# A weight load released by GpSimd, behind a drain, instead of by TensorE

## The chip, the cores and the metric

The kernel runs on one core of one Trainium2 chip. The metric is the device time of one execution in microseconds (us). Three runs of the kernel before took 1146.43, 1149.06 and 1155.12 us, so its time is the median, 1149.06 us.

## What is computed

One decoder layer on x of 8 x 256 tokens with 512 features, all in float32: attention with a window mask, a long convolution over a second input, and a mixture of experts. Only the last part matters here. In the reference, shortened:

```python
idx, wts = _router(x, gate_w, e_bias)            # 64 experts, 6 for each token
shared = _relu2(x @ shared_up_w.T) @ shared_down_w.T
# routed: each expert takes at most CAP = 128 tokens
h  = _relu2(einsum('ecd,eid->eci', xd, w1))      # 512 -> 256
yd = einsum('eci,edi->ecd', h, w2)               # 256 -> 512
out = x + shared + zeros((T, D)).at[tok].add(y_assign)
```

## The kernel before

The program is written engine by engine: each engine has its own list of instructions in the order in which it runs them, and semaphores tie the lists together. Nothing is planned at run time.

The expert stage is the last one. It handles 64 experts, one by one, in eight passes of a loop over UE = 8 experts (s is the place in the pass, i the pass). For each expert n = 8 i + s:

- SyncE (SP) issues one load of the expert's weights, 1 MB, into slot n mod 4 of the ring `wring` (NW = 4 slots). The line is 382.
- GpSimd (POOL) gathers the 128 token rows of the expert from `token_rows` into a ring of eight slots with an indirect DMA (line 515), eight experts ahead of their use.
- TensorE transposes the token rows (line 1466), multiplies them with the first weights (`hidden`), waits for ReLU and square, and multiplies with the second weights (`outputs`). Its order in a step is `tokens_T` of the expert after next, `hidden` of the next expert, `outputs` of this one, and in four of the eight steps a part of one tile of the shared network (`tile_part`).
- VectorE scales the result by the gates into `ysb`, which has two slots, and copies the row numbers for the scatter (lines 1192 to 1194).
- GpSimd adds the 128 result rows into `out` in device memory with an indirect DMA that accumulates (line 526). Two such transfers may touch the same row, so each waits until the one before has landed (semaphore `added`). Once in a pass it adds a tile of the shared network's rows in the same way (`scatter_tile`, line 533). That makes 64 + 8 such row transfers, one behind the other. Between two of them GpSimd issues one gather.

GpSimd's order in the loop is, for s = 0 to 7: `scatter` of the next expert, `gather(s)`; with s = 7 `scatter_tile` goes first. `scatter` tells VectorE, by `scatter_landed`, that the transfer before has landed, and VectorE then refills the `ysb` slot.

The weight load of expert n waits, before the change, on the semaphore of TensorE's `outputs` of expert n - 4, which is the last reader of the slot:

```python
sp.wait_ge(y_filled[(s - NW) % UE], i + (s // NW + 1))
```

At the end of the block every engine gets a drain, which the trace books to line 72 (`with ctx:`). GpSimd has another one ahead of its first selection (line 397).

Of the kernel before, what the change touches and what calls it, by code (L numbers as in the profile page):

```python
# [60 lines left out]
def program(nc, a, out):  # L61
    f32, u32 = mybir.dt.float32, mybir.dt.uint32
    ALU, ACT, AX = mybir.AluOpType, mybir.ActivationFunctionType, mybir.AxisListType
    V, G, A, TE = nc.vector, nc.gpsimd, nc.scalar, nc.tensor
# [7 lines left out]
    with ctx:  # L72
# [3 lines left out]
        def sem(name):  # L76
            return ctx.enter_context(nc.semaphore(name))
# [85 lines left out]
        NW = 4  # L163
# [32 lines left out]
        UE = 8  # L196
# [60 lines left out]
        y_filled = [sem(f"expert_out_slot{k}_filled") for k in range(UE)]  # L257
# [3 lines left out]
        tile_ready = sem("shared_tile_ready")  # L261
        added = sem("rows_added_to_the_result")
        scatter_landed = sem("scatter_landed")
        out_written = sem("result_rows_begun")


# [68 lines left out]
        @block.sync  # L335
        def _(sp):
            sp.dma_start(X[:, 0:4, :], a["x"][0:4 * P, :].rearrange("(t p) d -> p t d", p=P)).then_inc(x_loaded, 16)

            for s in (*empt, *conv_used, *conv_filled, *y_filled, *y_ready, hsq_ready, tile_ready):
                sp.sem_inc(s, 1)  # L340
            sp.sem_inc(scatter_landed, 3)
            sp.sem_inc(conv_done, 2)
            sp.sem_inc(x_loaded, 16)

            sp.wait_ge(tables_loaded, 16 * 4)
            with sp.Fori(1, PAIRS) as i:

                sp.wait_ge(x_loaded, i * 16 + 16)
                sp.dma_start(X[:, ds(i * 4, 4), :],
                             a["x"][ds(i * (4 * P), 4 * P), :].rearrange("(t p) d -> p t d", p=P)).then_inc(x_loaded, 16)  # L350

            sp.wait_ge(consts_ready, 1)
            sp.dma_start(out[T:ROWS, :], zeros[:]).then_inc(zero_written, 16)
            sp.dma_start(xrows[T:ROWS, 0:D], zeros[:]).then_inc(zero_written, 16)
            sp.dma_start(xrows[T:ROWS, D:XW], zeros[:, 0:E]).then_inc(zero_written, 16)
            sp.wait_ge(pad_ready, 1)
            sp.dma_start(toep[:], kpad[:]).then_inc(toep_written, 16)

            sp.wait_ge(full[FA1.bank(("vlo",))], FA1.filled(("vlo",)))
            sp.wait_ge(toep_written, 16)  # L360
            toep_v = bass.AP(toep.tensor, 1, [[P + D, SH], [1, P], [1, D]])
            with sp.Fori(0, SH // NTR) as i:
                for s in range(NTR):

                    sp.wait_ge(conv_filled[s], i + 1)
                    sp.wait_ge(toep_written, 16)
                    sp.dma_start(tring[:, s:s + 1, :], toep_v[ds(i * NTR + s, 1), :, :].rearrange("h p d -> p h d"))\
                      .then_inc(head_loaded[s], 16)
                    sp.dma_start(cring[:, s, :, :].rearrange("p m i -> p (m i)"),
                                 a["ctxE"][ds((i * NTR + s) * P, P), :]).then_inc(head_loaded[s], 16)  # L370

            for k, t in enumerate(TILES3):
                sp.wait_ge(x3_ready[k % NX], k // NX + 1)
                sp.dma_start(xrows[t * P:(t + 1) * P, 0:D], x3[:, k % NX, :]).then_inc(x3_written[k % NX], 16)
            sp.wait_ge(gates_ready, 1)
            sp.dma_start(xrows[0:T, D:XW].rearrange("(t p) c -> p t c", p=P), W).then_inc(gates_written, 16)
            with sp.Fori(0, E // UE) as i:
                for s in range(UE):

                    sp.wait_ge(y_filled[(s - NW) % UE], i + (s // NW + 1))  # L380
                    sp.wait_ge(gates_ready, 1)
                    sp.dma_start(wring[:, s % NW, :], a["wexp"][ds((i * UE + s) * P, P), :])\
                      .then_inc(wexp_loaded[s % NW], 16)

            sp.wait_ge(added, 16 * (E + NT // 2))
# [3 lines left out]
        def _(pool):  # L389
# [130 lines left out]
            def scatter(s, i, before):  # L520

                pool.wait_ge(y_ready[s % 2], i * (UE // 2) + (s // 2 + 2))
                if before is not None:
                    pool.wait_ge(added, before)
                    pool.sem_inc(scatter_landed, 1)  # L525
                pool.indirect_dma_start(out, bass.IndirectOffsetOnAxis(ap=idxs[:, s % 2:s % 2 + 1], axis=0),  # L526
                                        ysb[:, s % 2, :], None, compute_op=ALU.add).then_inc(added, 16)

            def scatter_tile(i):
                pool.wait_ge(tile_ready, i + 2)  # L530
                pool.wait_ge(added, i * (16 * (UE + 1)) + 16 * UE)
                pool.sem_inc(scatter_landed, 1)
                pool.indirect_dma_start(out, bass.IndirectOffsetOnAxis(ap=idxt[:, 0:1], axis=0),
                                        ytile, None, compute_op=ALU.add).then_inc(added, 16)
# [4 lines left out]

            pool.wait_ge(out_written, 16 * 3)  # L540
            scatter(0, 0, None)
            with pool.Fori(0, last) as i:
                for s in range(UE):

                    if s == UE - 1:
                        scatter_tile(i)
                    scatter((s + 1) % UE, i + (s + 1) // UE, i * (16 * (UE + 1)) + 16 * (s + 1 + (s + 1) // UE))
                    gather(s)
            for s in range(UE - 1):
                scatter(s + 1, last, last * (16 * (UE + 1)) + 16 * (s + 1))  # L550
# [1037 lines left out]
```

## Time and profile before

| what | value |
|---|---|
| time, median of three runs | 1149.06 us |
| time of the profiled execution | 1150.28 us |
| its span in the trace | 1148.5 us |
| mean granted TensorE clock | 0.93 of 2.4 GHz |
| first row transfer starts | 693.04 us |
| last row transfer starts | 1142.05 us |
| row transfers (lines 526 and 533) | 72 |
| TensorE busy in the pass from 918 to 976 us | 48.57 of 58 us |

The profiled execution's own time is its span and 1.8 us around it. The expert stage, from the first row transfer to the end, is 455 us of the span. What happens between two row transfers can be read on GpSimd's own time line, since it issues them.

### The profile page before, as it was taken

Reading aid. Unit: us, or ns where it says so; the run is one execution under the profiler, and the core shown is the slowest. Engines: PE = TensorE matmul, PEld = TensorE weight load, DVE = VectorE, ACT = ScalarE, POOL = GpSimd, SP = SyncE. Lnnn points to the kernel's source line nnn. Section 1 sums busy time; section 2 is a strip of 40 time slices with the busy share of each in tenths; the row PEclk is TensorE's granted clock in tenths of the full one; section 3 lists DMA queues with packets and bytes.
Section 4 is the critical chain, followed back from the end, with each engine's and each line's share of the span. In section 5 each row is a group of like instructions: output and inputs, shape, how many; then the busy total and the mean of one; then the engine's idle time right before and its main releaser. Section 6 shows DMA issues by size and latency. Waiting matters only on the chain. (4 is left out here: it accounts for less than half of the span.)

```text
span 1148.5 us, 14772 instructions
## 1 busy us (share of the span) xinstructions
PE 972.9 (85%) x4721; PEld 663.7 (58%) x4721; DVE 632.7 (55%) x1362; ACT 256.4 (22%) x787; POOL 429.1 (37%) x354
## 2 busy tenths in 40 slices
PE   3697989979879999977999989999797979797961
PEld 2365555656566666657744347767474746574740
DVE  3787786876369999997499943212222222221210
ACT  1282552825331111111311002111111111111100
POOL 2344260432336666643015023343434343443322
PEclk9798999989899999995899999999898989898986
DMA  7200000002043233302304037989797979887943
GB/s 273 75 1 1 0 0 0 0 1 65 1 156 110 80 83 85 87 1 92 129 0 165 37 120 223 262 244 258 200 264 193 250 203 243 222 266 200 259 96 46
DMA packets 44686, 143.18 MB, mean 125 GB/s; under 512 B 7345, under 2 KB 11697, under 8 KB 35697
## 3 DMA queue, kind: packets, MB, share of 16 engines
q1 hardware_dynamic: 25392, 91.35, 23.2%
q0 software_dynamic: 15488, 37.76, 17.5%
q10 hardware_dynamic: 3776, 13.70, 3.1%
q8 instruction: 16, 0.26, 0.1%
q14 instruction: 14, 0.11, 0.0%
HBM read 114.36 MB, written 28.43 MB: 124 GB/s over the span
## 5 line engine op out<-in xcount | busy, mean ns | idle before, releaser
L1236 PE MATMUL ps<-arena 128*128 128x128 f32 (+3 forms) x2560 | 632.1, 402 | 77.1 <-DVE arena L1178 53.8
L1236 PEld LDWEIGHTS ps<-arena 128*128 128x128 f32 x2560 | 403.1, 194 | 255.0 <-issue 149.5
L526 POOL DMA_INDIRECT out<-arena,scatter_rows x64 | 100.6, 1572 | 238.1 <-DMA out<-arena,scatter_rows 176.9
L1192 DVE COPY scatter_rows<-slot_rows_u 128x1 uint32 (+1 forms) x64 | 9.8, 154 | 313.1 <-POOLq L525 234.2
L1236 PE MATMUL ps<-features_T,arena 128*128 (+2 forms) x640 | 115.1, 338 | 0.0
L431 POOL TENSOR_TENSOR arena<-arena 128x512 f32<-128x512 f32 x48 | 49.2, 1053 | 164.6 <-DVE arena L773 164.5
L571 ACT ACTIVATE arena<-ps 128x512 f32<-128x512 f32 (+2 forms) x148 | 82.1, 573 | 123.2 <-DVE residual L1144 61.2
L1236 PEld LDWEIGHTS ps<-features_T,arena 128*128 128x128 f32 x640 | 83.9, 192 | 37.3 <-issue 37.3
L515 POOL DMA_INDIRECT arena<-token_rows,gather_rows x64 | 65.2, 1018 | 71.9 <-DVE gather_rows L1171 52.7
L581 ACT ACTIVATE arena<-arena 128x128 f32<-128x128 f32 x192 | 74.0, 387 | 66.1 <-DVE arena L761 66.1
L738 ACT ACTIVATE arena<-ps 128x256 f32<-128x256 f32 x64 | 24.5, 383 | 285.4 <-PE ps L1236 257.7
L946 DVE TENSOR_TENSOR arena<-ps,arena 128x256 f32<-128x256 f32 x128 | 74.6, 623 | 8.2 <-issue 5.0
L470 POOL TENSOR_TENSOR arena<-arena 128x512 f32<-128x512 f32 x32 | 40.8, 1274 | 83.4 <-DVE arena L954 83.4
L461 POOL TENSOR_TENSOR arena<-arena 128x1024 f32<-128x1024 f32 x32 | 60.6, 1892 | 0.0
L1501 PE MATMUL ps<-arena 128*128 128x512 f32 x128 | 57.5, 592 | 0.0
L855 DVE TENSOR_TENSOR arena<-arena 128x128 f32<-128x128 f32 (+1 forms) x48 | 48.8, 1075 | 11.1 <-ACT arena L571 11.1
L1466 PEld LDWEIGHTS ps<-ident,arena 128*128 128x128 f32 x256 | 33.0, 147 | 29.5 <-issue 28.8
L949 DVE TENSOR_TENSOR arena<-ps,arena 128x224 f32<-128x224 f32 (+2 forms) x96 | 48.7, 507 | 0.0
L1255 PE MATMUL ps<-features_T,arena 128*128 128x512 f32 x96 | 45.8, 621 | 3.4 <-DVE features_T L870 2.3
L1194 DVE TENSOR_SCALAR arena<-ps,arena 128x512 f32<-128x512 f32 x64 | 48.0, 750 | 0.8 <-issue 0.3
L1178 DVE TENSOR_TENSOR arena<-arena 128x256 f32<-128x256 f32 x64 | 26.8, 418 | 36.8 <-ACT arena L738 33.4
L695 ACT ACTIVATE arena<-features_T 128x256 f32 x32 | 13.3, 415 | 137.7 <-DVE arena L954 135.7
(160 smaller groups left out, 999.0 us busy)
## 6 DMA issues: line engine op xcount, KB each, us to landing
arena<-wexp SPq DMA_DIRECT2D x64, 1024.0 KB
arena<-toeplitz_rows SPq DMA_DIRECT2D x32, 256.0 KB, 3.1
arena<-ctxE SPq DMA_DIRECT2D x32, 192.0 KB, 3.3
residual<-x SPq DMA_DIRECT2D x4, 1024.0 KB, 5.8
token_rows<-arena SPq DMA_DIRECT2D x16, 256.0 KB, 2.0
arena<-suT ACTq DMA_DIRECT2D x1, 2048.0 KB, 7.8
arena<-sdT ACTq DMA_DIRECT2D x1, 2048.0 KB, 12.7
out<-residual ACTq DMA_DIRECT2D x1, 2048.0 KB, 7.6
```

What stands on the lines that cost most here:

```text
L431: G.tensor_tensor(e, e, rinv[:, b, 4 * c:4 * c + 4, q:q + 1].broadcast_to((P, 4, P)), ALU.mult)\
L461: G.tensor_tensor(kvb[:, s, :, 0:32].rearrange("p m (d i) -> p m d i", d=4), c[:, :, 0:SD].unsqueeze(2).broadcast_to((P, DC * B, 4, SD)), ...
L515: pool.indirect_dma_start(xg[:, s, :], None, xrows, bass.IndirectOffsetOnAxis(ap=idxg[:, s:s + 1], axis=0))\
L526: pool.indirect_dma_start(out, bass.IndirectOffsetOnAxis(ap=idxs[:, s % 2:s % 2 + 1], axis=0), ysb[:, s % 2, :], None, compute_op=ALU.add) ...
L571: A.activation(dst, src, ACT.Copy, **kw).then_inc(empt[bank], 1)
L581: ins = A.activation(prob[:, b, k, q, :], prob[:, b, k, q, :], ACT.Exp, bias=negmax[:, b, k, q:q + 1], scale=1.0, accum_out=rowsum[:, b, k ...
L855: V.tensor_tensor(heads(dst[:, m, :])[:, :, lo:lo + 16], heads(src[:, m, :])[:, :, hi:hi + 16], sin[:, lo:lo + 16].unsqueeze(1).broadcast_ ...
L946: V.tensor_tensor(pr[:, :, :, :, d], y[:, :, :, 8 * d:8 * d + 8], q[:, :, :, d:d + 8], ALU.mult)
L949: V.tensor_tensor(pr[:, :, :, d:8, 3 + d], y[:, :, :, 8 * d:8 * d + 8 - d], q[:, :, :, 0:8 - d], ALU.mult)
L1194: V.tensor_scalar(ysb[:, s % 2, :], ps[:, 4 + s % 2, :], xg[:, s, ds(i * UE + (D + s), 1)], None, ALU.mult)\
L1236: ins = TE.matmul(out_ap, lhsT, rhs, start=(n == 0), stop=(n == len(pairs) - 1))
L1501: ins = TE.matmul(ps[:, 7, :], htile[:, k, :], sdT[:, k, :], start=(k == 0), stop=(k == 7))
```

## The change

The load of expert n's weights no longer waits on TensorE's `outputs` of expert n - 4. GpSimd gets a drain behind each expert's row transfer, whose completion raises a new semaphore `scatter_begun`, and the load waits for that of expert n - 4. The semaphore starts at NW = 4, so that the first four loads wait for nothing. `scatter_tile` gets no drain. No load, gather or row transfer is added or taken away.

```diff
+        scatter_begun = sem("scatter_descriptors_written")
...
+            sp.sem_inc(scatter_begun, NW)
...
             with sp.Fori(0, E // UE) as i:
                 for s in range(UE):
-                    sp.wait_ge(y_filled[(s - NW) % UE], i + (s // NW + 1))
+                    sp.wait_ge(scatter_begun, i * UE + (s + 1))
                     sp.wait_ge(gates_ready, 1)
                     sp.dma_start(wring[:, s % NW, :], a["wexp"][ds((i * UE + s) * P, P), :])\
                       .then_inc(wexp_loaded[s % NW], 16)
...
                 pool.indirect_dma_start(out, bass.IndirectOffsetOnAxis(ap=idxs[:, s % 2:s % 2 + 1], axis=0),
                                         ysb[:, s % 2, :], None, compute_op=ALU.add).then_inc(added, 16)
+
+                G.drain().then_inc(scatter_begun, 1)
```

## Rows read from the trace of the kernel before

**Rows 1.** The page's costliest groups: busy, mean ns | idle before, by what ended.

```profile
L526 POOL DMA_INDIRECT out<-arena,scatter_rows x64 | 100.6, 1572 | 238.1 <-DMA out<-arena,scatter_rows 176.9
```

**Rows 2.** Waits between 720 and 1140 us: us in total, times, longest.

```profile
POOL out L526 <- DMA out<-arena,scatter_rows: 171.7, 49, 7.1
PE ps L1236 <- DVE arena L1178: 53.8, 23, 8.3
SPq L382 <- PE ps L1236: 342.6, 54, 11.7
```

**Rows 3.** Busy time by stretches: PE, PEld, DVE, ACT, POOL, clock, DMA share, GB/s.

```profile
918.00:976.00 58.00, 48.57 (x270) 34.35 (x270) 12.70 (x36) 8.22 (x18) 22.45 (x17) 0.94 0.84 225
```

**Rows 4.** Time line of GpSimd: the first two row transfers; tile transfers of passes one and seven.

```profile
693.04 1.61 POOL L526 DMA_INDIRECT out<-arena,scatter_rows  x1 [10.21 <-DVE arena L1194]
700.55 1.58 POOL L526 DMA_INDIRECT out<-arena,scatter_rows  x1 [5.90 <-DVE arena L1194]
...
746.13 1.57 POOL L533 DMA_INDIRECT out<-arena,tile_scatter_rows  x1 [3.50 <-DMA out<-arena,scatter_rows]
...
1090.40 1.57 POOL L533 DMA_INDIRECT out<-arena,tile_scatter_rows  x1 [5.33 <-DMA out<-arena,scatter_rows]
```

**Rows 5.** Time line of GpSimd around two row transfers, a quick and a slow one.

```profile
982.86 1.55 POOL L526 DMA_INDIRECT out<-arena,scatter_rows  x1 [3.97 <-DMA out<-arena,tile_scatter_rows]
984.72 1.02 POOL L515 DMA_INDIRECT arena<-token_rows,gather_rows  x1 [0.30 <-issue]
988.28 1.57 POOL L526 DMA_INDIRECT out<-arena,scatter_rows  x1 [2.55 <-DMA out<-arena,scatter_rows]
...
877.85 1.57 POOL L526 DMA_INDIRECT out<-arena,scatter_rows  x1 [2.59 <-DMA out<-arena,scatter_rows]
879.73 1.01 POOL L515 DMA_INDIRECT arena<-token_rows,gather_rows  x1 [0.31 <-issue]
886.57 1.57 POOL L526 DMA_INDIRECT out<-arena,scatter_rows  x1 [5.83 <-DMA out<-arena,scatter_rows]
```

**Rows 6.** Time line of SyncE's queue: single issues of weight loads near rows 5.

```profile
981.01 0.33 SPq L382 DMA_DIRECT2D arena<-wexp  x1
...
877.16 0.33 SPq L382 DMA_DIRECT2D arena<-wexp  x1
```

**Rows 7.** Stretches of 1 us behind the load of 981.01, columns as in rows 3.

```profile
982.00:983.00 1.00, 1.00 (x10) 0.85 (x8) 0.00 (x0) 0.00 (x0) 0.14 (x1) 1.00 0.84 172
983.00:984.00 1.00, 0.05 (x1) 0.00 (x0) 0.00 (x0) 0.84 (x2) 1.00 (x1) 1.00 1.01 426
984.00:985.00 1.00, 0.00 (x0) 0.00 (x0) 0.00 (x0) 0.03 (x1) 0.69 (x2) 1.00 1.06 406
985.00:986.00 1.00, 0.00 (x0) 0.00 (x0) 0.00 (x0) 0.00 (x0) 0.74 (x1) 1.00 0.94 96
```

**Rows 8.** Time from issue to landing, of line 526, then of line 533.

```profile
DMA to landing us min/median/max: 4.4/5.1/9.2
...
DMA to landing us min/median/max: 4.6/4.9/6.7
```

**Rows 9.** Time line of GpSimd at the end: no gathers or loads any more.

```profile
1103.51 1.57 POOL L526 DMA_INDIRECT out<-arena,scatter_rows  x1 [4.08 <-issue]
1108.66 1.55 POOL L526 DMA_INDIRECT out<-arena,scatter_rows  x1 [3.58 <-DMA out<-arena,scatter_rows]
...
1142.05 1.55 POOL L533 DMA_INDIRECT out<-arena,tile_scatter_rows  x1 [4.21 <-issue]
```

**Rows 10.** Instructions of line 532 and 72: duration ns min/median/max, first and last start.

```profile
L532 POOLq EVENT_SEMAPHORE  x8: 17/17/5226, 745.4 to 1136.1; - x8
...
L72 POOLq EVENT_SEMAPHORE  x2: 17/17/17, 1148.3 to 1148.3; - x2
L72 POOLq DRAIN  x1: 6394/6394/6394, 1141.8 to 1141.8; - x1
L72 SPq COMPARE_BRANCH  x1: 38/38/38, 1146.6 to 1146.6; - x1
```

**Rows 11.** GpSimd's drain of line 397, and what stands on both sides of it.

```profile
L397 POOLq DRAIN  x1: 3547/3547/3547, 1.0 to 1.0; - x1
...
4.34 0.13 POOL L396 IOTA tile_rows<- 128x8 f32 x1
4.69 0.29 POOL L398 TENSOR_SCALAR_AFFINE_SELECT ident<-ident 128x128 f32<-128x128 f32 x1 [0.22 <-issue]
```

## The prediction

> **What bounds the kernel now.** I read the page's costliest groups first. GpSimd's row transfers of line 526 stand with 238 us of idle time in front of them, 177 us of it ended by the landing of another row transfer [rows 1]. The waits of the expert stage say the same: in 420 us GpSimd waits 172 us for row transfers, TensorE some 54 us for VectorE, and SyncE 343 us for TensorE [rows 2]. SyncE's wait is no loss, it only says that loads are held back. TensorE is busy for 48.6 us of a pass of 58 us [rows 3], so it is the second limit, about 9 us behind. The first limit is the chain of row transfers: issue, landing, next issue. From the tile transfer of the first pass to that of the seventh there are six passes of nine row transfers: (1090.40 - 746.13) / 6 = 57.4 us a pass, 6.38 us a transfer [rows 4].
>
> What one link is made of can be seen at 982.86 us: 1.55 us of GpSimd's work, a gap of 0.3 us, a gather of 1.02 us, then idle until 988.28 us, 5.42 us after the start [rows 5]. A transfer lands 4.4 to 9.2 us after its start, 5.1 us in the middle [rows 8]. The turn from a landing to the next start is read where a wait's end is shown: the last long wait of line 532 ended at 1136.1 + 5.2 = 1141.3 us, and the transfer behind it started at 1142.05 us, so 0.75 us [rows 9, 10]. So a link is landing time + 0.75 us, and the gather is free: it lies under the landing. Without loads and gathers the seven links from 1103.51 to 1142.05 us take 5.5 us each [rows 9], a landing time of 4.75 us.
>
> The landing time depends on where a weight load falls. With the load issued 1.85 us before the transfer (981.01 and 982.86 us), the link took 5.42 us; with it 0.69 us before (877.16 and 877.85 us), the link took 8.72 us [rows 5, 6]. A load takes the DMA engines at 400 to 430 GB/s about 2 to 4 us behind its issue [rows 7], and 1 MB at that rate is 2.5 us. A row transfer whose descriptors come while a load is moving is held up.
>
> **The change, part by part.** (1) The wait of the load. A load gets a later release, from `outputs` of expert n - 4 to the row transfer of expert n - 4, which can't start before that result was computed and scaled. On SyncE's queue only later loads and the last wait for the row transfers stand behind it. It moves nothing by itself while the weights still come in time, which I check below.
>
> (2) The drain. This is the step that decides. It stands on GpSimd behind each expert's row transfer. Queued behind it are the gather, the next wait on `added`, the signal `scatter_landed` to VectorE and the next row transfer; who waits for it are SyncE's load and, through the chain, everybody. What does a drain behind an indirect DMA cost? The trace has one, at the end. The last row transfer starts at 1142.05 us and GpSimd's own work on it ends 1.55 us later, at 1143.60 us [rows 9]. The drain runs from 1141.83 us (1141.8 in its row) for 6.39 us, to 1148.2 us, and GpSimd's next event follows at 1148.3 us; SyncE, which waits for the landing of the same transfer, passes at 1146.6 us [rows 10]. So the drain did not end with the descriptors, but 4.6 us later and 1.6 us after the landing. A drain with compute in front of it is another matter: that of line 397 ended at 1.0 + 3.55 = 4.5 us, within 0.1 us of the end of the IOTA at 4.47 us [rows 11]. I conclude that GpSimd's drain waits for its DMAs in flight, and that it costs nothing of its own.
>
> Beside that stands a rule that speaks the other way. The Trainium skill, page "PSUM — Partial Sum Buffer", section "Engine vs sequencer instructions", says that a drain waits until the engine is fully idle, and its page "Perfetto Trace Analysis", section "DMA Instruction — SWDGE (GPSIMD)", that the profiler's end of such an instruction is the last descriptor written, not the data moved. Taken together they would put the end of the drain at the end of the 1.55 us; the row of the exit drain disagrees, and by them the time would be that of the first rival.
>
> How long the drain stays beyond the landing has two ends: 0, if it ends with the transfer, and 1.6 us, the exit drain's. The exit drain is the nearest row, but it had 136 GpSimd transfers in front of it and no drain of DMAs among them, while a drain in the loop has at most two; the drain of line 397 shows no fixed cost. If the 1.6 us are clearing up of what has gathered, little is left for each. I take 0.2 us, and keep 1.6 us as a rival and for the range.
>
> (3) The gather. It stands behind the drain, so it no longer lies under the landing. After the drain GpSimd has to turn to it (0.75 us, as from any wait), work on it for 1.02 us, and go on to the next row transfer (0.3 us): 2.07 us where the link had 0.75 us. That is +1.3 us a link, for the 56 links with a gather.
>
> (4) The phase of the load. It is released by the drain, so some 0.2 us behind the drain's end, and the next row transfer starts 2.07 us behind it: 1.9 us after the load's issue. That is the phase of 981.01 and 982.86 us, where the landing took 5.42 - 0.79 = 4.6 us. But now the gather is issued between them and moves its rows ahead of the row transfer. Bounds: 4.6 us, if the gather costs nothing there, and 6.5 us, if the transfer is held up as much as half of the clash at 877.85 us (8.72 - 0.75 = 8.0 us). A gather is 128 rows of 2304 bytes, 0.3 MB, 0.7 us at 420 GB/s, which added to 4.6 us gives 5.3 us. I take 5.3 us.
>
> (5) Are the weights in time? A load is issued about 5.3 + 0.2 + 0.2 = 5.7 us behind the start of row transfer n - 4 and is in 4 to 5 us later [rows 7], at 10.5 us. `hidden` of n and `outputs` of n - 1 (two steps of about 2 us), scaling and start of transfer n - 1 need 5 to 6 us more: 16 us. Transfer n - 1 is due three links after n - 4, 22 us. The slack of 6 us also covers a tile part of 3.7 us. TensorE works 48.6 us a pass, the new pass is 66 us, so it is no limit either, at its full clock or at its short half-clock stretches.
>
> The sum. A link behind an expert's transfer in the loop: 5.3 + 0.2 + 2.07 = 7.6 us. The link behind a tile transfer has no drain and no gather: 4.9 + 0.75 = 5.7 us [rows 8]. A pass: 8 x 7.6 + 5.7 = 66.5 us, against 57.4 us: +9 us. The first transfer of each pass follows the tile link with neither load nor gather in front of it and lands in 4.8 us, which takes 0.5 us off: +8.6 us. Seven passes lie in the loop: +60 us. The seven links of the end get 0.2 us each and four of them a load: +3 us. Nothing changes before 693 us. On the profiled execution's 1150.3 us this gives 1213 us; it is 1.2 us above the median of the runs, so 1212 us.
>
> **The rivals.** (a) The drain ends with the descriptors, 1.6 us behind the start. Then the gather still lies under the landing, and the loads are issued 1.9 us behind each row transfer, 3.7 us ahead of the next, always in the same phase: the load runs between two row transfers. Landing 4.9 us, the link 5.7 us instead of 6.4 us, over some 63 links 44 us less, a few of them lost to TensorE's tile parts and late weights (the slack is then 3 x 5.7 - 13 = 4 us): 1110 us. For it: the name of the semaphore describes what a drain could do. Against it: the exit drain's 6.39 us. It decides from the moment the drain's end comes before about 4 us behind the transfer's start. Chance 0.10.
>
> (b) The drain costs the full 1.6 us beyond the landing each time. 8 x 1.4 us more a pass, 78 us: +139 us over seven passes, +13 us at the end, 1302 us. For it: it is the only row of such a drain. Chance 0.22.
>
> (c) The drain waits, but the new order keeps every load clear of the row transfers, and the gather costs them nothing: 4.6 + 0 + 2.07 = 6.7 us a link, 8 x 6.7 + 5.7 = 59 us a pass, +12 us: 1162 us. This is at the edge of what the measurement can tell. Chance 0.08, half of it within 1%.
>
> (d) The change doesn't do what it says: if both signals come at the same time nothing moves. But the order of the code puts `outputs`, the scaling and the wait for the row transfer before between the old signal and the new one, so the loads do move. Under 0.02.
>
> **How the numbers follow.** The forecast has 0.58, with its own range of 1180 to 1245 us (landing time 4.9 to 6.0 us, drain 0 to 0.5 us beyond the landing). Rivals (b) and (c) lie on the same side. The range that should hold 8 in 10 reaches from rival (c) to rival (b): 1160 to 1306 us; (a) is left out, and the far side of (b). A measurement of this kernel tells about 1% from no change. Faster by over 1%: only (a), 0.10. Within 1%: half of (c) and what (a) loses to late weights, 0.05. Slower: 0.85.
>
> **What would show it.** GpSimd's drains of line 531 in the changed kernel lasting 3 us or more, to the landing of the row transfer, show step 2; 0.1 us each shows rival (a); their end against the landing gives the 0.2 or 1.6 us. Gathers that start 0.7 us behind the drain, with the next row transfer 1.3 us behind them, show step 3. Load issues 1.9 us ahead of a row transfer and landing times near 5.3 us show step 4; 6 us and more would mean that the gather, or a load drawn out by it, stands in front of the rows. TensorE waiting for weights with the row transfers waiting for VectorE would show step 5 wrong. The prediction is wrong above all if the exit drain's wait belongs to the end of the block and not to the DMA.

## The result, and the profile after

The changed kernel took 1202.91 us (median of four runs, 1195.74 to 1205.27), against 1149.18 us before: a ratio of 1.044, 95% interval 1.041 to 1.048. The forecast was 1212 us. Two later executions took 3460.33 us (one of four with the drain alone) and 2525.76 us (one of the kernel before beside it); the medians and ratios given here leave them out.

In the list of the costliest groups the waits have changed places. Before, the idle time stood in front of the row transfers [rows 1]; now it stands in front of the gather of line 517, which waits for a row transfer's landing, though its code has no such wait:

```profile
L517 POOL DMA_INDIRECT arena<-token_rows,gather_rows x64 | 65.3, 1020 | 302.7 <-DMA out<-arena,scatter_rows 219.2
L528 POOL DMA_INDIRECT out<-arena,scatter_rows x64 | 101.4, 1584 | 87.6 <-DMA out<-arena,tile_scatter_rows 31.3
```

The drain's own row says why (changed kernel, instructions of lines 531, 528 and 384 with their times to landing):

```profile
L531 POOLq DRAIN  x64: 4897/6001/6756, 692.2 to 1191.4; - x64
...
L528 POOL DMA_INDIRECT out<-arena,scatter_rows x64: 1552/1576/1745, 692.5 to 1191.6; - x64
...
DMA to landing us min/median/max: 4.5/5.1/5.8
...
L384 SPq DMA_DIRECT2D arena<-wexp x64: 332/333/940, 609.9 to 1172.6; - x64
...
DMA to landing us min/median/max: 4.6/4.8/12.5
```

All 64 drains take 4.9 to 6.8 us; the row transfers land after 4.5 to 5.8 us. One link on GpSimd's time line, the one load that SyncE issues in it, and its drain:

```profile
960.56 1.58 POOL L528 DMA_INDIRECT out<-arena,scatter_rows  x1 [0.30 <-issue]
966.46 1.01 POOL L517 DMA_INDIRECT arena<-token_rows,gather_rows  x1 [4.32 <-DMA out<-arena,scatter_rows]
967.78 1.59 POOL L528 DMA_INDIRECT out<-arena,scatter_rows  x1 [0.30 <-issue]
...
965.84 0.33 SPq L384 DMA_DIRECT2D arena<-wexp  x1
...
L531 POOLq DRAIN  x1: 5549/5549/5549, 960.1 to 960.1; - x1
```

The link is 7.22 us. The drain ends at 960.1 + 5.55 = 965.65 us, within 0.1 us of the row transfer's landing, 5.0 us behind its start. The gather, which stood 0.3 us behind the row transfer's own work [rows 5], now starts 0.62 us behind the load's issue, that is 0.8 us behind the drain, and the next row transfer 1.32 us later. The load is issued 1.94 us ahead of that transfer.

The tile transfers give the length of a pass, the last rows the end of the kernel (time line of GpSimd, changed kernel):

```profile
751.67 1.64 POOL L537 DMA_INDIRECT out<-arena,tile_scatter_rows  x1 [0.30 <-issue]
...
1141.28 1.58 POOL L537 DMA_INDIRECT out<-arena,tile_scatter_rows  x1 [0.30 <-issue]
1147.18 1.55 POOL L528 DMA_INDIRECT out<-arena,scatter_rows  x1 [4.32 <-DMA out<-arena,tile_scatter_rows]
...
1166.66 1.55 POOL L528 DMA_INDIRECT out<-arena,scatter_rows  x1 [5.06 <-DMA out<-arena,scatter_rows]
1173.30 1.55 POOL L528 DMA_INDIRECT out<-arena,scatter_rows  x1 [5.09 <-DMA out<-arena,scatter_rows]
...
1197.28 1.55 POOL L537 DMA_INDIRECT out<-arena,tile_scatter_rows  x1 [4.12 <-DMA out<-arena,scatter_rows]
```

A pass is (1141.28 - 751.67) / 6 = 64.9 us, where it was 57.4 us [rows 4]. The 7.5 us more, seven times, are 53 us. The whole chain of row transfers, first start to last, went from 449.0 us to 1197.28 - 692.45 = 504.8 us, 56 us more; the span grew by 54 us. The chain starts 0.6 us earlier than before, and from the start of the last transfer to the end of the span it is 4.92 us, where it was 6.45 us: the drain at the end of the block stays a shorter time beyond the last landing, as shown below.

### The profile page after: what moved, and what is told of

It is laid out like the page before. It is cut to its first block, busy times and chain, and to the rows that moved or that the text cites. A ratio compares the mean times of both kernels' runs of the same rounds, so it can differ in the third digit from the quotient of the medians.

```text
span 1202.2 us, 14885 instructions
## 1 busy us (share of the span) xinstructions
PE 996.1 (83%) x4721; PEld 683.8 (57%) x4721; DVE 636.9 (53%) x1362; ACT 256.6 (21%) x787; POOL 430.5 (36%) x354
## 4 chain that ended last, share of the span: by engine, by line
issue 30%; DVE 29%; PE 12%; POOLq 10%; POOL 5%; ACT 5%; DVEq 5%; DMA 4%; ACTq 0%
POOLq L531 10%; PE ps L1240 9%; DVE arena L950 4%; POOL arena L517 4%; ACT arena L585 4%; DVE arena L859 3%; DMA out<-arena,tile_scatter_rows 3%; DVE arena L953 3%; DVE arena L965 3%; DVE arena L1139 2%; DVEq L1143 2%; DVE arena L967 2%; DVE arena L757 1%; DVE arena L955 1%; DVEq L861 1%
## 5 line engine op out<-in xcount | busy, mean ns | idle before, releaser
L1240 PE MATMUL ps<-arena 128*128 128x128 f32 (+3 forms) x2560 | 649.7, 414 | 116.3 <-issue 57.2
L1240 PEld LDWEIGHTS ps<-arena 128*128 128x128 f32 x2560 | 423.1, 206 | 300.7 <-issue 211.7
```

The costliest lines, as they stand in the source:

```text
L1240: ins = TE.matmul(out_ap, lhsT, rhs, start=(n == 0), stop=(n == len(pairs) - 1))
```

## The experiments

Two questions were open: whether the drain or the later release of the loads costs the time, and what the release would be worth without the drain. Ratios are those of each kernel to the kernel before on the same chip, with 95% intervals.

**The drain alone.** The kernel before, plus one line.

```diff
                 pool.indirect_dma_start(out, ...).then_inc(added, 16)
+                G.drain()
```

> The kernel before with the drain alone: it raises nothing, and the loads keep their old release by TensorE. Theory A (the drain holds GpSimd until the row transfer has landed, and the gather behind it is laid bare): the turn from landing to the next start is 2.2 us as in the changed kernel, and the time is 1190 to 1225 us, most of the 54 us and perhaps more, since loads at any phase hold up some row transfers. Rival B (the later release of the loads costs the time): within 10 us of 1149 us.

Measured: 1197.06 us (median of three), ratio 1.036 (1.034 to 1.039). The drain takes a median of 5.79 us here as well, with a load that waits on TensorE as before:

```profile
L528 POOLq DRAIN  x64: 4695/5790/8170, 695.0 to 1183.3; - x64
```

Theory A holds, rival B falls: the drain alone makes most of the loss. The new release adds 0.8% to it (the intervals are apart). In the profiled executions the chain from first to last row transfer is 493.7 us with the drain alone and 504.8 us in the changed kernel. Of this difference 8 us lie in the six passes between tile transfers (63.6 and 64.9 us each) and 4 us in the end phase; the stretch before them is 1 us shorter. The end phase shows how the phase of the load (its place in time between two row transfers) enters: with no gather behind the drain, the load goes out only some 0.7 us ahead of the next row transfer, and links such as that from 1166.66 to 1173.30 us take 6.64 us, where the three with no load about take 5.7 to 5.9 us. What the 8 us in the passes are was not tested; the median landing is 4.9 us with the drain alone and 5.1 us in the changed kernel.

**The signal without the drain.** A tiny addition behind the row transfer carries the signal. It needs no landing: in the time line below it ends at 969.79 + 0.79 = 970.58 us, 0.2 us behind the end of GpSimd's own work on the row transfer (968.76 + 1.59).

```diff
-                G.drain().then_inc(scatter_begun, 1)
+                pool.wait_ge(scatter_begun, i * UE + (s + NW))
+                G.tensor_tensor(mark[:], zeros[:, 0:1], zeros[:, 1:2], ALU.add).then_inc(scatter_begun, 1)
```

(The wait only orders an addition behind the one before it.)

> The changed kernel with the drain replaced by an addition of 128 x 1 elements on GpSimd that raises the same semaphore, so that the signal comes when GpSimd is through with the descriptors and waits for no landing. Theory A: GpSimd issues the gather under the landing again, the loads go out about 2 us behind each row transfer and some 3.7 us ahead of the next, which then lands in 4.9 us; a link is 5.7 us and the time about 1110 us (1098 to 1130). Rival B: the release is as late as in the changed kernel by its order, so the time stays above 1149 us, towards 1200.

Measured: 1129.91 us, ratio 0.980 (0.975 to 0.984). Time line of GpSimd and of SyncE's queue in this kernel:

```profile
968.76 1.59 POOL L529 DMA_INDIRECT out<-arena,scatter_rows  x1 [2.46 <-DMA out<-arena,scatter_rows]
969.79 0.79 POOL L533 TENSOR_TENSOR mark<-zeros 128x1 f32<-128x1 f32 x1
970.74 1.02 POOL L518 DMA_INDIRECT arena<-token_rows,gather_rows  x1 [0.16 <-issue]
974.49 1.59 POOL L529 DMA_INDIRECT out<-arena,scatter_rows  x1 [2.72 <-DMA out<-arena,scatter_rows]
...
970.75 0.33 SPq L385 DMA_DIRECT2D arena<-wexp  x1
```

The gather is under the landing again, and the load is issued 1.99 us behind the row transfer and 3.74 us ahead of the next. That is rival (a)'s world, and it is faster than both kernels, though not by as much as expected. The same kernel once more, in five rounds:

> The kernel with the addition once more, beside the next one on the same chip: 0.976 to 0.984 of before.

Measured: 1131.05 us, 0.980 (0.977 to 0.984).

**Two other phases of the load.** First 1.3 us later, with the addition moved behind the gather:

```diff
             scatter(...)
-                (the addition, inside scatter)
             gather(s)
+            begun(...)      # the same wait and addition
```

> As the run before, but the addition stands behind the gather: the load goes out about 1.5 us later, 3.5 us behind the row transfer and 2.3 us ahead of the next. If the phase of the load sets the landing time, it rises to 5.3 to 5.6 us, a link to 6.2 us, the time to about 1135 us. If the gain of the run before comes from anything else than the phase, the two give the same time within 5 us.

Measured: 1157.67 us, ratio 1.002 (0.999 to 1.005). The phase matters, and more than expected in time: the chain of row transfers takes 456.9 us here and 421.2 us in the kernel before this one. Then 2 us earlier, at the dispatch of the row transfer:

```diff
-                G.drain().then_inc(scatter_begun, 1)
+                pool.sem_inc(scatter_begun, 1)
```

> The changed kernel without the drain; the semaphore is raised by GpSimd's sequencer right behind the dispatch of the row transfer, so that the load goes out with the start of the transfer and not 2 us behind it. If the time of the kernel with the addition (0.980 of before) came from the phase of the load, this loses it: the load moves while the rows are wanted, landing times are 5.5 to 7 us, a link 6.3 to 7.5 us, 1145 to 1215 us. If only the missing drain counts, it is within 10 us of that kernel, 1120 to 1140 us.

Measured: 1206.78 us, ratio 1.049 (1.044 to 1.055), as slow as with the drain and without one. The landing times of the expert row transfers, first with the signal behind the descriptors (load 2.0 us behind the transfer's start), then behind the gather (3.3 us), then at dispatch (0 us), each from its own kernel:

```profile
DMA to landing us min/median/max: 4.5/4.8/6.6
```

```profile
DMA to landing us min/median/max: 4.6/5.2/6.9
```

```profile
DMA to landing us min/median/max: 4.5/6.6/7.2
```

And a link at dispatch, 7.51 us long, with its load:

```profile
952.56 1.55 POOL L528 DMA_INDIRECT out<-arena,scatter_rows  x1 [3.98 <-DMA out<-arena,tile_scatter_rows]
954.42 1.02 POOL L517 DMA_INDIRECT arena<-token_rows,gather_rows  x1 [0.30 <-issue]
960.07 1.57 POOL L528 DMA_INDIRECT out<-arena,scatter_rows  x1 [4.63 <-DMA out<-arena,scatter_rows]
...
952.52 0.33 SPq L384 DMA_DIRECT2D arena<-wexp  x1
```

In this link the load lands first, 5.3 us behind its issue, and the rows 6.7 us behind theirs, 1.4 us later. Over the kernel the median landing of the rows is 1.8 us longer than with the load 2.0 us behind them. That the load's data are served ahead of the rows is the likely reason; the order inside the DMA engines was not looked at. Late weights are not the cause, since the idle time before the expert row transfers (us, times) ends with landings and hardly with late results:

```profile
  DMA out<-arena,scatter_rows: 237.1, 52
...
  DVE arena L1198: 13.2, 2
```

**The drain behind the gather.**

```diff
             scatter(...)
-                (the drain, inside scatter)
             gather(s)
+            G.drain().then_inc(scatter_begun, 1)
```

> The changed kernel with the drain and its signal behind the gather, so that the gather lies under the landing again, but the drain waits for both transfers. Theory A: the gather lands about 5.7 us behind the start of the row transfer, the turn behind the drain is 0.75 us, the load goes out 0.6 us ahead of the next row transfer, which then lands in 5.7 us: links near 7 us, the time 1170 to 1205 us. If the bare gather were no cost, the time would be that of the changed kernel, 1203 us, within 5 us.

Measured: 1223.32 us, ratio 1.058 (1.056 to 1.060), slower than the changed kernel and above the range that I had given. Time line of GpSimd, the drain of that link, all drains, and the gathers' time to landing:

```profile
970.77 1.57 POOL L528 DMA_INDIRECT out<-arena,scatter_rows  x1 [4.96 <-issue]
972.65 1.02 POOL L517 DMA_INDIRECT arena<-token_rows,gather_rows  x1 [0.30 <-issue]
978.22 1.59 POOL L528 DMA_INDIRECT out<-arena,scatter_rows  x1 [4.55 <-issue]
...
L532 POOLq DRAIN  x1: 6175/6175/6175, 971.1 to 971.1; - x1
...
L532 POOLq DRAIN  x64: 5011/6254/6907, 693.8 to 1210.4; - x64
...
DMA to landing us min/median/max: 3.7/4.5/7.3
```

The link is 7.45 us. The gather starts 1.9 us behind the row transfer and lands 4.5 us later, 6.4 us behind it; the drain waits for that and ends at 971.1 + 6.18 = 977.3 us, some 0.1 us beyond the gather's landing, and the next transfer starts 0.9 us behind the drain. What the gather wins by lying under the landing, it loses by being waited for. I had priced its landing at 5.7 us and the turn at 0.75 us.

**What a drain costs by itself.** A second drain behind each first:

```diff
+                G.drain()
                 G.drain().then_inc(scatter_begun, 1)
```

> The changed kernel with a second drain behind each first, which has nothing left to wait for. If a drain costs only what it waits for, the second adds about 0.1 us to each of 64 links and the time rises by 3 to 12 us. If a drain had a price of its own, as the 1.6 us of the exit drain beyond the landing would let one think, it rises by 50 to 100 us.

Measured: 1209.06 us, ratio 1.051 (1.045 to 1.056), 6 us more than the changed kernel by the medians, though the intervals of the two ratios overlap; a price of 50 us or more for a drain itself is ruled out. The first and the second drain of this kernel:

```profile
L531 POOLq DRAIN  x64: 4943/6060/6877, 691.7 to 1200.3; - x64
...
L532 POOLq DRAIN  x64: 47/47/47, 697.4 to 1205.3; - x64
```

With nothing in flight a drain takes 47 ns.

**The exit drain's 1.6 us.** The kernel before with a drain behind `scatter_tile`'s transfer alone:

```diff
                                         ytile, None, compute_op=ALU.add).then_inc(added, 16)
+                G.drain()
```

> The kernel before with one drain a pass, behind the tile's row transfer, and nothing else. Behind that transfer 16 or 17 GpSimd transfers have gathered instead of 136 in the kernel before and one or two in the changed one. If the time of a drain beyond the landing grows with what has gathered, it is 0.15 us in the changed kernel, 1.6 us at 136, and here 0.3 to 0.35 us; if the step is a matter of one or many, it is 1.6 us here too. The time rises by 0 to 12 us, for seven links of the 71.

Measured: 1157.10 us, ratio 1.005 (1.002 to 1.007). Its drains, and the landing of the transfers in front of them:

```profile
L535 POOLq DRAIN  x8: 5232/6095/10801, 745.2 to 1151.8; - x8
...
L533 POOL DMA_INDIRECT out<-arena,tile_scatter_rows x8: 1552/1574/1575, 745.1 to 1152.0; - x8
...
DMA to landing us min/median/max: 4.6/5.2/9.9
```

A drain starts 0.1 us ahead of its transfer (868.6 and 868.73 us in one pass), so it ends about 0.75 us behind the landing in the passes where 17 transfers stand since the drain before: more than the expected 0.35 us, less than 1.6 us. The first drain of this kernel, with 24 transfers in front of it, ends 1.0 us behind the landing (745.2 + 10.8 and 745.1 + 9.9), the last, with 10, about 0.4 us (1151.8 + 5.23 and 1152.0 + 4.6). The exit drains of the other kernels fit. In the changed kernel only one transfer stands between the last drain of the loop and the exit drain, which ends at 1197.1 + 4.79 = 1201.9 us, 0.1 us behind SyncE's passing the wait for the landing at 1201.8 us; in the kernel with the addition, which has no other drain of DMAs, it ran for 6.35 us again:

```profile
L72 POOLq DRAIN  x1: 4792/4792/4792, 1197.1 to 1197.1; - x1
L72 SPq COMPARE_BRANCH  x1: 38/38/38, 1201.8 to 1201.8; - x1
```

```profile
L72 POOLq DRAIN  x1: 6345/6345/6345, 1115.7 to 1115.7; - x1
```

So the time beyond the landing grows with the transfers issued since the last drain: 0.1 us at one to three, 0.4 us at 10, 0.75 us at 17, 1.0 us at 24, 1.6 us at 136. It is about 0.04 us a transfer up to 24, and less than in proportion at 136; what bounds it there was not tried.

**One link more for the weights.** The kernel with the addition still waits at times for results that are late:

```profile
POOL out L529 <- DMA out<-arena,scatter_rows: 112.3, 39, 4.4
...
POOL out L529 <- DVE arena L1200: 29.4, 8, 4.4
```

The ring lets the load of expert n follow row transfer n - 5, if TensorE is through with n - 4:

```diff
+            pool.wait_ge(y_filled[0], 2)
+            pool.sem_inc(scatter_begun, 1)
             scatter(0, 0, None)
...
+                if i is not last or s < UE - 1:
+                    pool.wait_ge(y_filled[(s + 1) % UE], i + ((s + 1) // UE + 2))
-                pool.wait_ge(scatter_begun, i * UE + (s + NW))
+                pool.wait_ge(scatter_begun, i * UE + (s + NW + 1))
                 G.tensor_tensor(mark[:], ...).then_inc(scatter_begun, 1)
```

> The kernel with the addition, with each load released one link earlier, by the addition behind row transfer n - 5, in front of which GpSimd also waits for TensorE's outputs of expert n - 4. The phase of the load is the same, but the weights have 6 us more. If the 20 us that the kernel with the addition missed its 1110 us by are TensorE's late results, waiting on weights, the late links vanish and the time is 1105 to 1122 us. If they are landing times, it stays within 4 us of 0.980 of before.

Measured: 1118.54 us, ratio 0.970 (0.964 to 0.976). Again in five rounds, on one chip with the kernel with the addition:

> The kernel with the addition and the release one link earlier once more: 0.965 to 0.976 of before. If the 1% between the two is real, their intervals are apart here; if it was the chip, they overlap for the most part.

Measured: 1124.90 us, ratio 0.974 (0.970 to 0.978), against 0.980 (0.977 to 0.984) for the other: lower by 0.6 to 1% in both rounds, but the intervals overlap slightly, so a gain over the kernel with the addition is likely and not shown. What ended the idle time before the row transfers, in the second run of the kernel with the addition 34.5 us for VectorE's late results, in 8 places, has gone down (the first run of the new kernel):

```profile
  DVE arena L1205: 8.6, 2
```

So the late results did become fewer. But the profiled executions of the two need the same time from first to last row transfer, 421 us each (1115.95 - 694.72 and 1112.21 - 690.66 us), and differ in when the first starts. The execution profiled of the kernel with the addition was also its quickest both times (1124.10 us with a median of 1129.91 us, 1121.51 us with one of 1131.05 us). So the profile doesn't show where the medians' 6 to 11 us lie, nor that the late results cost them, and that stays open. This is the fastest kernel of the study, 2.6 to 3.0% ahead of the kernel before.

## Why the prediction was right, step by step

- **Step 1**, the later release moves nothing by itself: nearly. The drain alone gave 1.036 and the change 1.044, so beside the drain the release costs 0.8%, and 11 us of the chain in the profiled executions, most of it in the passes.
- **Step 2**, the drain waits for the DMAs in flight: right, shown in 64 drains of 4.9 to 6.8 us and by the second drain's 47 ns. The exit drain was the row that decided. Taking 0.2 us beyond the landing instead of that row's 1.6 us was right too (0.1 us), for the reason given: with one drain a pass it is 0.75 us. A drain in the loop has up to three transfers in front of it (gather, tile transfer, row transfer), and not at most two as the prediction says; it ends 0.1 us beyond the landing there too.
- **The rule that spoke the other way.** The Trainium skill, page "PSUM — Partial Sum Buffer", section "Engine vs sequencer instructions", has a drain wait until the engine is fully idle. Here the drains lasted to the landing, about 3 us and more beyond the end of GpSimd's 1.58 us of work, so for GpSimd "idle" must count its transfers in flight. The measurement decides.
- **Step 3**, the gather laid bare: right. 0.8 us to turn, 1.01 us of work and 0.3 us give 2.1 us, forecast 2.07 us.
- **Step 4**, the phase: the load is 1.94 us ahead of the next row transfer, forecast 1.9 us. The landing time was 5.1 us in the middle, forecast 5.3 us. This is the term that was too big, and the drain's 0.2 us was 0.1 us. Behind an expert's transfer a link came out at 7.35 us in the mean and not at (66.0 - 5.7) / 8 = 7.54 us, eight times a pass; the link behind a tile transfer gives some back, with 6.2 us in the mean of six (5.6 to 6.7 us) instead of 5.7 us. A pass came out at 64.9 us and not at 66.0 us. From the first row transfer to the seventh tile transfer the change added (1141.28 - 692.45) - (1090.40 - 693.04) = 51.5 us where the forecast had 60 us, nearly all of the 9 us that it was too high. The forecast's own range was put too narrow above: landing 6.0 us and drain 0.5 us together are +1.0 us on 56 links, so its upper end should have been some 1270 us and not 1245 us.
- **Step 5**, weights in time: right for the chain. TensorE does wait for weights, but the next row transfer stands ready 0.3 us behind the gather all the same.
- **The end**: forecast +3 us, measured (1197.28 - 1147.18) - (1142.05 - 1096.56) = 50.1 - 45.5 = +4.6 us. The forecast left some 1.6 us for four loads; three links with a load 0.7 us ahead of the row transfer are about 0.8 us longer each than those with none, 2.4 us. Against that, the exit drain gave back 1.5 us, which the forecast did not count.
- **The rivals.** (a), a signal at the end of the descriptors, did not happen in this change, but its mechanism is real: built with an addition, it gave 1130 us, not the 1110 us worked out. Late results (29 us of waits) and single landings of up to 6.6 us stand in its profile, but where the 20 us lie is not shown: with most of the late results gone, the next kernel's chain took the same 421 us. (b) and (c) did not happen.

## What to carry to other kernels

A drain on GpSimd behind its DMAs was a wait for their landing here: look up in the trace which transfers the drains follow, how long they last and how much stands in front of them, before putting one into a loop, and ask what work behind it loses its cover. To signal that descriptors are written, attach the signal to a small instruction of the same engine behind the transfer. Where a chain of small transfers runs beside big loads, try the moment at which each load is released: here it was worth several per cent, in both directions, though no byte was added or saved.

## What was not expected of the hardware

The steepness of the phase. The same loads, one for each row transfer, released 0, 2.0 and 3.3 us behind its start, gave 1.049, 0.980 and 1.002 of the time before, with median landings of 6.6, 4.8 and 5.2 us. Within 2 us of release time lies a difference of 7% of the whole kernel, more than the change under study made.

And how long a drain stays beyond the landing: 0.1, 0.4, 0.75, 1.0 and 1.6 us with 1 to 3, 10, 17, 24 and 136 transfers since the last drain; with none in flight a drain takes 47 ns.
